# A recommender tower on one core: gathers of 128 rows with one transfer out, splits two chunks ahead, and another order of the first chunk

## What is computed

```
e    = stack([tbl_f[ids[:, f]] for f in range(39)])           # 512 x 39 x 16
z0   = einsum('bid,bjd->bdij', e, e)                          # all pairs of fields, for each of the 16 columns
cur0 = relu(einsum('bdk,kl->bld', z0, W0))                    # 1521 -> 128
next_h, direct0 = split(cur0, 2)                              # 64 each
z1   = einsum('bid,bjd->bdij', e, next_h)                     # 39 x 64 products
cur1 = relu(einsum('bdk,kl->bld', z1, W1))                    # 2496 -> 128
z    = sum(concat(direct0, cur1), axis=-1)                    # 192 per sample
y    = relu(relu([z, dense] @ W_top1 + b1) @ W_top2 + b2) @ W_top3
```

## Time and profile before

| | |
|---|---|
| median of 3 runs | 440.63 us (438.06 to 440.85) |
| the profiled execution | 439.21 us, span 437.2 us |
| TensorE busy | 406.2 us, 93% of the span |
| VectorE busy | 347.9 us, 80% |
| ScalarE busy | 225.6 us, 52% |
| GpSimd busy | 284.5 us, 65%, its last gather about seven tenths of the way through |
| granted clock, mean | 0.986 |

### The profile page before, as it was taken

One profiled execution on the slowest core, in us unless ns is written; L12 is line 12 of the kernel. 1 busy time (PEld: TensorE's weight loads), 2 busy tenths in 40 slices (PEclk: granted clock), 3 DMA queues, 4 the chain that ended last, 5 costly groups with the idle time before them and its releaser, 6 DMA issues.

```text
span 437.2 us, 4204 instructions
## 1 busy us (share of the span) xinstructions
PE 406.2 (93%) x1490; PEld 250.0 (57%) x1490; DVE 347.9 (80%) x196; ACT 225.6 (52%) x224; POOL 284.5 (65%) x180
## 2 busy tenths in 40 slices
PE   0587699799999999999999999999999999998897
PEld 0454356456566656565656565665656565665464
DVE  0304664799999998989898989898989898999900
ACT  2115445365655647483747464738374656553422
POOL 5778887888888888888888888888888100000000
PEclk9989899899999999999999999999999999999999
DMA  8383549594848383838384747475675638350000
GB/s 284 107 195 61 127 107 224 137 219 135 209 122 220 92 235 77 237 82 222 107 222 122 220 116 208 120 201 142 164 179 155 183 116 220 105 184 0 1 0 2
DMA packets 25524, 64.04 MB, mean 146 GB/s; under 512 B 7779, under 2 KB 15928, under 8 KB 19743
## 3 DMA queue, kind: packets, MB, share of 16 engines
q1 hardware_dynamic: 19156, 60.76, 51.4%
q0 software_dynamic: 5632, 1.35, 2.9%
q10 hardware_dynamic: 715, 1.66, 1.1%
HBM read 59.88 MB, written 3.85 MB: 146 GB/s over the span
## 4 chain that ended last, share of the span: by engine, by line
PE 78%; POOL 12%; issue 4%; DMA 3%; DVE 2%; ACT 0%; DVEq 0%; ACTq 0%
PE acc L497 16%; POOL found L276 12%; PE acc L529 12%; PE acc L521 12%; PE acc L522 12%; PE acc L540 10%; PE sums L480 6%; PE acc L536 4%; PE spread L510 3%; DMA found<-in_table_dram,rows_sb 2%; PE spread L569 2%; DVE z_lo L419 2%; DVE z L411 1%; DMA base_sb<-in_base_dram 1%; PE sums L558 1%
## 5 line engine op out<-in xcount | busy, mean ns | idle before, releaser
L276 POOL DMA_INDIRECT found<-in_table_dram,rows_sb x176 | 284.3, 1615 | 56.7 <-issue 53.4
L319 ACT ACTIVATE z_hi<-z 128x2048 fp32r<-128x2048 f32 x64 | 122.4, 1913 | 82.6 <-DVE z L411 82.6
L419 DVE TENSOR_TENSOR z_lo<-z,z_hi 128x2048 fp32r<-128x2048 f32 x64 | 146.2, 2285 | 14.6 <-ACT z_hi L319 14.6
L521 PE MATMUL acc<-z_hi,w_hi 128*128 128x512 f32 x256 | 106.8, 417 | 5.4 <-ACT cur L312 3.1
L497 PE MATMUL acc<-squares,w 128*128 128x512 f32 (+1 forms) x224 | 110.8, 612 | 0.0
L411 DVE TENSOR_TENSOR z<-x_wide,h 128x2048 f32<-128x2048 f32 x48 | 109.6, 2282 | 0.0
L522 PE MATMUL acc<-z_hi,w_lo 128*128 128x512 f32 x256 | 100.9, 394 | 0.0
L411 DVE TENSOR_TENSOR z<-spread,h 128x2048 f32<-128x2048 f32 x32 | 73.1, 2286 | 20.9 <-ACT h L303 16.8
L295 ACT ACTIVATE squares<-sums 128x1024 f32<-128x1024 f32 x64 | 58.4, 913 | 58.9 <-PE sums L480 58.9
L529 PE MATMUL acc<-z_lo,w_hi 128*128 128x512 f32 x256 | 82.2, 443 | 0.6 <-DVE z_lo L419 0.6
L529 PEld LDWEIGHTS acc<-z_lo,w_hi 128*128 128x128 f32 x256 | 48.0, 189 | 24.1 <-issue 15.1
(11 more groups left out here) (44 smaller groups left out, 146.3 us busy)
## 6 DMA issues: line engine op xcount, KB each, us to landing
x_wide<-x_rows SPq DMA_DIRECT2D x48, 512.0 KB, 4.5
x_wide<-x_rows SPq DMA_DIRECT2D x80, 256.0 KB, 5.2
x_parts<-x_rows SPq DMA_DIRECT2D x32, 128.0 KB, 2.6
x_wide<-x_rows SPq DMA_DIRECT2D x16, 192.0 KB
found<-in_table_dram,rows_sb POOLq DMA_INDIRECT x176
x_rows<-found SPq DMA_DIRECT2D x32, 80.4 KB
w_sb<-in_w_dram SPq DMA_DIRECT2D x1, 1280.0 KB, 6.6
x_rows<-found SPq DMA_DIRECT2D x16, 73.1 KB
```

Of the source, the lines that this page charges most:

```text
L276: pool.indirect_dma_start(out=found[:, b, 2, s * D:s * D + D], out_offset=None, in_=table, in_offset=bass.IndirectOffsetOnAxis(ap=rows_sb[ ...
L319: nc.scalar.activation(z_hi[:, n % RING], z[:, n % RING], ACT.Copy).then_inc(hi_done, 1)
L419: nc.vector.tensor_tensor(z_lo[:, n % RING], z[:, n % RING], z_hi[:, n % RING], ALU.subtract).then_inc(lo_done, 1)
L521: nc.tensor.matmul(acc1[:, :], w1_hi[:, t, :], z_hi[:, r, a, :], start=(t == 0), stop=False)
```

## The change

The ids arrive as 128 partitions by 17 blocks of 10 numbers, the first block being the starts of the tables. The 40 times 32 rows of a chunk (the last field twice) are dealt out as 128 partitions by 10, so a chunk takes 10 gathers of 128 rows. `lay_out` writes them with one DMA of 128 partitions. The separate transfer of the starts (`base`) and the one that filled row 39 of `x_rows` are gone, with the wait on it. In the program order, `split(1)` moves ahead of `evict0(0)` and `multiply(0)`; `split(c + 2)` stands in the first group of chunk c; both reduces stand ahead of the last `low_part`; the first chunk has an order of its own on TensorE, ScalarE and VectorE; and on SyncE `widen(1, 0)` moves ahead of `bring(2)`. The core of the diff:

```diff
-                for s, w in enumerate(SET_COLS):
-                    start = x_rows[b, 0, 0, GW * s:GW * s + 1]
-                    sp.dma_start(bass.AP(start.tensor, start.offset, [[N, F], [FR * N, 3], [1, w]]),
-                                 found[F * s:F * s + F, b, :, 0:w]).then_inc(rows_out[b], 16)
+                start = x_rows[b, 0, 0, 0:1]
+                sp.dma_start(bass.AP(start.tensor, start.offset, [[GW, P], [FR * N, 3], [1, GW]]),
+                             found[:, b, :, :]).then_inc(rows_out[b], 16)
...
-            sp.wait_ge(filler_in, 16)
             bring(0)
             widen(0, 0)
             widen(0, 1)
             bring(1)
             widen(0, 2)
+            widen(1, 0)
             bring(2)
-            for c in range(CHUNKS - 1):
+            widen(1, 1)
+            widen(1, 2)
+            for c in range(1, CHUNKS - 1):
+                if c + 2 < CHUNKS:
+                    bring(c + 2)
                 for i in range(len(WIDE)):
                     widen(c + 1, i)
-                if c + BUFS < CHUNKS:
-                    bring(c + BUFS)
...
-            act.dma_start(base_sb[:, :], base).then_inc(ids_in, 16)
             act.dma_start(select_in, select).then_inc(select_in_done, 16)
-
-            filler = x_rows[0, 0, F, 0:1]
-            act.dma_start(bass.AP(filler.tensor, filler.offset, [[3 * FR * N, BUFS], [FR * N, 2], [1, N]]),
-                          select[0:2 * BUFS, 0:N].rearrange("(b h) n -> b h n", h=2)).then_inc(filler_in, 16)
...
+            split(1)
             evict0(0)
-            split(1)
             high_part(0)
-            high_part(1)
-            square(ND)
-            square(ND + 1)
...
-                    if g == G - 1 and c + BUFS < CHUNKS:
-                        split(c + BUFS)
+                    if g == 0 and 0 < c < CHUNKS - 2:
+                        split(c + 2)
...
+                    if n == 3:
+                        split(2)
                     if n + 1 < G * CHUNKS:
                         multiply(n + 1)
+                    if g == G - 1 and c + 1 < CHUNKS:
+
+                        reduce0(c + 1)
+                        if c:
+                            reduce1(c - 1)
                     if is_v(n):
                         low_part(n)
...
+            add_up(ND)
+            contract1_hi(0)
+            add_up(ND + 1)
+            contract0(ND)
+            contract1_lo(0)
+            contract1_hi(1)
+            spread_out(3)
+            add_up(ND + 2)
+            contract0(ND + 1)
+            contract1_lo(1)
+            add_up(ND + 3)
+            contract0(ND + 2)
+            contract1_whole(2, ND + 3)
+            spread_out(G)
+            contract1_hi(3)
+            contract1_lo(3)
+            contract1_hi(4)
```

More of the change, by code:

```diff
@@ L362, in _ @@
                         evict1(c - 1)
+                    if g == 0 and c < 2:
+                        square(ND * (c + 1))
+                    if n == 0:
+                        high_part(1)
+                    if g == 0 and c < 2:
+                        square(ND * (c + 1) + 1)
                     if g < 2 and c + 1 < CHUNKS:
                         square(ND * (c + 1) + 2 + g)
-                    if g > 2 and c + 2 < CHUNKS:
+                    if g > 2 and 0 < c < CHUNKS - 2:
                         square(ND * (c + 2) + g - 3)
@@ L459, in _ @@
                         reduce0(0)
-                    if n == 1:
-                        split(2)
-                    if g == 1 and c:
-                        reduce1(c - 1)
-                    if g == G - 1 and c + 1 < CHUNKS:
-                        reduce0(c + 1)
-                    if g == G - 1 and c + BUFS < CHUNKS:
-                        split(c + BUFS)
+                    if g == 0 and 0 < c < CHUNKS - 2:
+                        split(c + 2)
+                    if n == G * (CHUNKS - 1) + 1:
+                        reduce1(CHUNKS - 2)
             reduce1(CHUNKS - 1)
@@ L641, in layout @@
     tables = [np.ascontiguousarray(inputs[f"tbl_{f}"]) for f in range(F)]
[L643 to L648 removed]
+    fields = list(range(F)) + [F - 1]
+    starts = np.cumsum([0] + [t.shape[0] for t in tables])[fields].astype(np.int32)
+    by_slot = np.zeros((P, 1 + CHUNKS, SLOTS), np.int32)
+    by_slot[:, 0] = np.repeat(starts, CB).reshape(P, SLOTS)
+    for c in range(CHUNKS):
+        by_slot[:, 1 + c] = ids[c * CB:c * CB + CB, fields].T.reshape(P, SLOTS)
     from_w0 = np.asarray(inputs["L0_rec_W0"]).reshape(F, F, P)
```

58 lines of the change are left out of this document (23 added, 35 removed).

## The result

The changed kernel takes 444.77 us in the median (442.58 to 445.82, 4 runs), the kernel before 440.48 us (4 runs): a ratio of 1.0116 with a 95% interval of 1.0087 to 1.0145. It is slower by 1.2%, where I had forecast 435.8 us, 1.1% faster. The profiled execution took 445.06 us, its span 443.2 us against 437.2.

What follows compares the result with a forecast made beforehand. The prediction took TensorE's own work to bound the steady part; only the start, first chunk and last chunk could move. -1.0 - 5.7 + 2.2 + 0.7 = -3.8 took the execution from 439.21 to 435.4, forecast as 435.8 us, range 432.5 to 439.

Steps and rivals of the forecast that it cites:

- The steady part: The eleven steady chunks, bound by TensorE's own work at 22.88 us a chunk: change of 0 predicted.
- the cover of 0.7 us: Steady chunks: low_part(36) would end at 247.5, TensorE wants it at 248.28, so the moved split costs nothing.
- the slower case: Rival: ScalarE's half of split(c + 2) late, TensorE waits for low_part(5c+1) in each of 13 chunks; 445 us, chance 0.08.
- fill a wait of 1.15 us: Steady chunks: the reduces moved ahead of low_part(5c + 4) take up a 1.15 us wait that VectorE has there.
- The start: Up to multiply(0): fewer gathers and earlier w0b give -1.0 us (-0.4 to -1.4); first add_up at 25.4 to 26.0.
- the COPY that I took as the bound: Start, VectorE: split(0) stands behind the COPY at 19.00, so it moves from 19.80 to 19.28 and no more.
- The clock holds: Rival: start keeps its clock (-1.5) and first chunk shows no spell (-2.2): 432 us, with one 433.5 to 434; chance 0.17.
- A gather of 128 rows: Start: its unseen time was bounded by 1.00 us (no growth) and 1.09 us (in proportion to rows).
- The first chunk: From multiply(0) to hi(5): the new order gives -5.7 us at full clock, +2.2 back for half-clock spells.
- The clock: TensorE at half clock behind waits: 1.5 us a spell, one and a half spells taken for the first chunk.
- The last chunk: VectorE sets the end; reduce1(13) now ahead of low_part(74) puts one reduce of 0.67 on the path: +0.7 us.
- The gain is given back in the first chunk: Rival: split(1) waits for 20 gathers and holds evict0(0) by 0.5 to 2.8 us; 437 to 439 us, chance 0.27.

Runs made afterwards that it cites:

- e8: e4 plus split(c + 2) in the first group of chunks 1 to 13, two chunks ahead: 432.63 us, ratio 0.9876 to the kernel before.
- e9: e4 plus both reduces moved ahead of low_part(5c+4), splits left in place: 434.47 us, ratio 0.9888 to the kernel before.
- e4: Kernel before with only ids in the new layout, ten gathers of 128 rows and one transfer out; old orders, base and filler kept: 432.47 us, ratio 0.9885.
- e17: e8 plus the new order of the first chunk on all engines: 437.82 us, ratio 0.9940 to the kernel before.
- e13: e4 with the new start: 459.09 us, a time that says nothing of its edit because ScalarE stood still several times in the first 80 us.

## Why the prediction was wrong

**The steady part, predicted 0, measured +8.2.** This is the step that failed. I looked at the cover of 0.7 us for the split itself; by itself the new place costs nothing, as e8 shows (22.86 us a chunk). I wrote that "the gathers are chunks ahead", and gave the slower case 0.08 for a late split. The place was right, the reason for lateness was another, and the lead was never counted. It stood in the rows: the earlier trace rows has 284.5 us of GpSimd in 180 instructions, and with the 0.30 us ahead of each gather that is 284.5 + 176 x 0.30 = 337 us, all the time until its last gather at 340. The 65% of the span hid an engine with nothing but these 0.30 us between its gathers. The second failure is in the same step: that the reduces ahead of low_part(5c + 4) "fill a wait of 1.15 us" was costed as free for VectorE, and it was; but the reduce and the split that stood behind low_part(5c+4) had been places at which gathers passed. With both gone from between low_part(5c+4), multiply(5c+6) and low_part(5c+5), one gather takes 7.2 us and the rate falls to 9 in 22.88 us, where 10 are needed. With either of the two left there the rate is 11 (e8, e9).

Of the 8.2 us, the first long chunk has 0.3, the next four about 1.0 each, and the last, 26.58, has 3.7: its gather landed later still, so that split(12) waited 2.69 us on ScalarE, TensorE waited 1.83 us to 297.75, and the clock went to half at 298.19 us. Behind it VectorE and GpSimd stood otherwise to one another, the next gather beside low_part(5c+4) passed, and thirteen were started between these two `cur` (timeline of the changed kernel):

```profile
308.32 2.29 DVE L416 TENSOR_TENSOR z_lo<-z,z_hi 128x2048 fp32r<-128x2048 f32 x1
309.15 2.27 POOL L275 DMA_INDIRECT found<-in_table_dram,rows_sb  x1 [0.30 <-issue]
```

**The start, predicted -1.0, measured -0.38.** `w0b` landed at 11.23 us, 3.5 earlier and not 0.4, but the gathers began 2.1 us later, since the ids landed later beside `select`. I had taken their landing as unchanged. So the first add_up ran at 26.28 us, behind a wait of 2.12 us for `x_parts`, where I had 25.4 to 26.0 and no wait. With the ids in halves multiply(0) came at 35.66, -3.5 against before and more than I had thought possible: the COPY that I took as the bound moved forward too, and the stretch of half clock at 28 us is gone. That stretch is the larger part: in e4, without it, it is 10.8 us from the first add_up to multiply(0), before 12.6. The first half of my rival "The clock holds" came true there, not in the changed kernel.

**A gather of 128 rows.** Bounded by 1.00 and 1.09 us, measured 0.94 us when nothing disturbs it: below both bounds. The price was no danger; the rate beside VectorE was.

**The first chunk, predicted -5.7 + 2.2 = -3.5, measured -3.0, for a wrong reason.** Timeline of the changed kernel, TensorE; the last row is hi(5):

```profile
68.37 1.20 PE L529 MATMUL acc<-z_lo,w_hi 128*128 128x512 f32 x4 [2.47 <-DVE z_lo L416]
...
71.17 1.22 PE L480 MATMUL sums<-x_parts,select_sb 128*128 128x512 f32 x2 [1.60 <-ACT squares L294]
...
77.71 0.80 PE L521 MATMUL acc<-z_hi,w_hi 128*128 128x512 f32 x1
```

Here hi(5) stands at +38.95 behind multiply(0), where I had 36.3 at full clock plus 2.2, and the two waits are those forecast (2.5 and 1.6 us where I had 2.9 and 1.9). The wait for `x_parts` that I called gone is still there: 2.33 us, to 43.22, +4.46 where I had +2.7, since split(1) waited for its gathers and `lay_out(1)` was issued at 37.58, -1.2 and not -2.6. But with the old order hi(5) runs at 72.78 in e4, +36.59, and at 72.61 in e8, +36.43. The gain of this part is that of ten gathers for eleven, which shorten the wait of split(3) ahead of evict1(0) and leave one stretch of half clock behind multiply(0) for two; the new order gives 2.4 to 2.5 us of it back, 3.5 in e17 against e8. That the sum came out within 0.5 us of the measurement is luck as far as the change's orders go: my sum compared the new order with the kernel before as it was, and never the old order with ten gathers.

**The clock.** I took 1.4 to 1.5 us for a stretch of half clock. Each lasts 3.4 us here (two in a row 6.8), which is 1.7 us where TensorE is the bound throughout. Until 110 us the changed kernel has three (one at 28, two in a row at 70 us), as many as the kernel before, e4 and e8 have one. The changed kernel has two more behind that. The rule of the Trainium skill that I had cited (TensorE: Matmul & The Clock Gate, What's actually happening) is borne out at 69.49 us, where the clock fell 1.1 us behind the wait of 2.5 us, and not at 43 us in the same kernel, where a wait of 2.33 us brought no stretch; in e8 three waits of 2.3, 1.5 and 1.1 us brought one stretch.

**The last chunk, +0.7 predicted, +0.6 measured.** The moved reduces are the cause: e9, which has them on top of e4, is 0.6 us longer there, e8 is not. But both the changed kernel and e9 have a stretch of half clock there (404 and 391 us) that the kernel before, e4 and e8 have not, and 0.7 us was counted without one; the agreement is partly chance.

**The rivals.** "The gain is given back in the first chunk" had its wait: split(1) waited 1.44 us for the gathers. But it had ended at 37.12 us when evict0(0) could go, at 37.52, and held up `x_parts` of chunk 1 only. The 0.6 us by which multiply(0) missed the forecast come from the first add_up. "Slower" named the right place and a time of 445 us, with the wrong cause and a chance of 0.08. (The shares of the chances give 0.46 for faster and 0.47 for within 1%; I had them the other way round.)

## What to carry to other kernels

An engine's share of the span says little on whether it paces: add its own gaps between instructions and look how long it goes on without any other. Where two engines interfere, moving short operations off a place changes how much of the other engine's work gets through there, even if the mover's own time is unchanged; count, at each use, how many units of the producer are ready and how many are needed, since a rate that is short by one shows only when the lead is gone. Sum each part of a change on top of the others and also alone: here ten gathers alone gain 1.2%, and the orders around them were worth nothing (the splits, the reduces, each alone) or less (the two together, the first chunk).

## What the runs showed of the hardware

- A gather (0.94 us for 128 rows, 1.00 for 117, each with 0.30 us ahead) beside a VectorE operation with both inputs in SBUF ends 0.8 to 0.9 us after that operation's end and takes 1.9 to 3.0 us. The exceptions are 20 gathers, most of them in e4 and e13, that began within 0.04 us of the operation's start: they took 0.94 or 0.95 us, and the operation 2.33 to 2.36 in place of 2.28. Beside a multiply whose first input is the spread in PSUM, or beside a reduce and done before the next operation holds it, it takes 0.94 to 1.00 us. The Trainium skill says the same of the pair (SBUF — State Buffer, Who interferes with whom: an operation with two SBUF inputs contends with GpSimd's reads, a reduce never), but infers there that writing a transfer's descriptors is not held up by such an operation. The gathers here are held, though it is not shown by which port.
- Some gathers are held over two or three operations that follow one another without a pause, 4.2 to 4.7 us and 7.1 to 7.4 (7.7 to 7.8 when begun in the reduce ahead). Of the gathers of before that began in an operation with another such behind it, 49 passed at its end and 1 did not; after, 28 and 11. A gather begun 0.31 us into low_part(5c+4) was held, one begun 0.83 us into it passed; yet 13 gathers begun 0.2 to 0.3 us into the multiply behind that of the spread passed at its end too. What decides it is open: neither the reduce directly ahead, nor an operation of 0.17 us in the run or ahead of it, nor the moment of the start alone does.
- The landing of a small transfer of ids (85 KB) moves by 2 us with what another queue issues at the same moment: used at 5.25 us beside `select` (changed kernel), at 3.37 us with `select` 0.45 us behind it (e4).
